# Preparing the first row tiles of a layer's attention within the last expert tiles of the layer before

## The chip, the cores and the metric

The kernel runs on one core of one Trainium2 chip, in one launch. The metric is the device time in microseconds of that core, the median of the timed runs. A profile of one execution by the hardware profiler stands beside it; its engines are TensorE (PE, with its weight loads as PEld), VectorE (DVE), ScalarE (ACT), GpSimd (POOL) and the DMA queues of SyncE (SP) and GpSimd. "Granted clock" is the share of TensorE's full clock that the chip grants: in this profile 1.00 (2.4 GHz) or 0.50 (1.2 GHz).

## What is computed

Two decoder-like layers on x of 4 x 1024 x 256 with a context of 4 x 77 x 256, in float32. Layer 0 is a cross attention and a mixture of experts; layer 1 a cross attention and a low-rank feed forward.

```python
def reference(x, ctx_1024, ...):
    x = x + _L0_xattn_ref(_layernorm(x), ctx_1024, ctx_1024, ...)
    x = x + _L0_ffn_ref(_layernorm(x), router_w, w1, w2)     # 8 experts, 2 chosen for a row, hidden 1024, gelu
    x = x + _L1_xattn_ref(ctx_1024, ctx_1024, _layernorm(x), ...)
    x = x + _L1_ffn_ref(_layernorm(x), U1, V1, b1, U2, V2, b2)
    return x

def _L1_xattn_ref(values, keys, query, Wv, Wk, Wq, Wo, bo):   # 16 heads of 16
    ...
    energy = jnp.einsum('nqhd,nkhd->nhqk', q, k)
    attention = jax.nn.softmax(energy / jnp.sqrt(jnp.float32(EMBED)), axis=-1)
    out = jnp.einsum('nhql,nlhd->nqhd', attention, v).reshape(N, Lq, EMBED)
    return out @ Wo.T + bo
```

## The kernel before

The 4096 rows of x are 32 row tiles of 128 (`NT`), eight for each of the four batches (`TB`). The function `experts_and_attend` holds layer 0's experts and layer 1's attention as one block: each engine runs its own written order of work, and semaphores join them. There is no planner; the order is that of the loops.

**Expert tiles.** Rows are gathered by expert. After seven short tiles come 32 full tiles (`FULL`) of 256 rows, `step(t)` on each engine. On TensorE one is four groups `up(0..3)` of twelve matmuls of 256 columns, two groups `down`, the transposes of the next tile's rows (`rows_turned`), and two more groups `down`. ScalarE applies the gelu to each up group (L1787) and copies the result y out (L1802); VectorE splits each activation into a high and a low half (L1908, L1910) and the turned rows too (L1897). GpSimd gathers the rows of a tile two tiles ahead (L1381), SP stores y (L1460).

**Row tiles of the attention.** The result of the experts for row tile f is two gathers from the stored y by GpSimd (`gather(f)`, L1406), a load of x by SP (L1465), and VectorE's `rows_in_full(f)`: two weighted additions, then mean and variance (L1969 to L1979). The gathers of rows 0 to 7 need only what the first tiles stored; `gather(TB)`, row 8, waits for the store of the last expert tile. GpSimd computes the deviation (`deviation(f)`, L1413, L1416), ScalarE normalizes (`normed_rows`, L1831), TensorE transposes (`rows_transposed`, L1692), ScalarE and VectorE keep the high and low halves (`high` L1825, `low` L1984). Then come four score matmuls of 308 columns (`scores(f, i)`, L1622), 16 heads in all, of which VectorE takes the maxima over the keys. The maxima of four row tiles make a group; they are scaled (L2002), transposed (`maxima_transposed`, L1631) and copied (L1858).

`SOON_ROWS` = 6 row tiles (`AHEAD`) are prepared up to `low` within expert tiles 25 to 31: `LED` is 25, `rows_in_full` of row t - 25 and the transposes of row t - 26 stand in tile t. X of these six has its own place; X of the others lies in the area of the experts' weights.

**The steps.** `STEPS` runs k from -5 to 32. Step k in 0 to 31 takes one quarter of a group g = k // 4: `scores_by_key(k)` (L1653, three terms, then the maxima as a fourth), the exponentials `exps(k, 0)` and `exps(k, 1)` by ScalarE (L1837), and in the next step `values` (L1665) and their copy (L1843). Beside this run the scores of row k + 5 (from row 5 on), `rows_in_full(k + 7)`, the normalization and transposes of row k + 6, and, from step 5 on, the heads and the projection of row k - 5. Steps -5 to -1 hold only the scores of rows 0 to 4 (`EARLY`), all four into the four banks of `sT_ps`, one reduction over all four by VectorE (`early_maxima`, L1994), and ten matmuls of `awake` (L1698), which compute nothing and keep TensorE occupied. Steps 0 to 4 have twelve `awake` matmuls each. On ScalarE, `normed_rows(k + 6)` stands in front of `exps(k, 0)`; on VectorE `rows_in_full(k + 7)` stands between reductions 1 and 2 of row k + 5.

The tail of GpSimd's order is:

```python
for t in range(LED, FULL):
    f = t - LED
    if f >= 3:
        deviation(f - 3)
    step(t)
    gather(f)
gather(SOON_ROWS + 1)
for f in range(FULL - LED - 3, SOON_ROWS):
    deviation(f)
```

and after it, for each row f from 6 on: `gather(f + 2)`, `deviation(f)`, and from f = 8 on the bias of row f - 8. So the gathers of row 8 stand ahead of the deviation of row 6.

## Time and profile before

| | us |
|---|---|
| median of three timed runs | 1009.81 |
| lowest and highest | 1009.03, 1011.61 |
| the profiled execution | 1009.16 |
| its span | 1007.2 |
| TensorE busy (share) | 918.5 (91%) |
| VectorE busy | 616.9 (61%) |
| ScalarE busy | 513.6 (51%) |
| GpSimd busy | 423.6 (42%) |

How to read it: the span is what the profiler saw from the first to the last instruction, and the execution's own time lies 2 us above it. Busy times overlap, and they are averages over stages with different limits; TensorE's matmuls are pipelined and their ends modelled, so the distance from one start to the next tells the cost of one in a row of them, and the duration (longer) doesn't. In a timeline the columns are start, duration, engine, line and operation, output and inputs with their shapes, the count of instructions merged into the row, and in brackets the idle time of the engine just before it and what ended that.

### The profile page before, as it was taken

Reading aid. Unit: us, or ns where it says so; the run is one execution under the profiler, and the core shown is the slowest. Engines: PE = TensorE matmul, PEld = TensorE weight load, DVE = VectorE, ACT = ScalarE, POOL = GpSimd, SP = SyncE. Lnnn points to the kernel's source line nnn. Section 1 sums busy time; section 2 is a strip of 40 time slices with the busy share of each in tenths; the row PEclk is TensorE's granted clock in tenths of the full one; section 3 lists DMA queues with packets and bytes.
Section 4 is the critical chain, followed back from the end, with each engine's and each line's share of the span. In section 5 each row is a group of like instructions: output and inputs, shape, how many; then the busy total and the mean of one; then the engine's idle time right before and its main releaser. Section 6 shows DMA issues by size and latency. Waiting matters only on the chain. (4 is left out here: it accounts for less than half of the span.)

```text
span 1007.2 us, 24069 instructions
## 1 busy us (share of the span) xinstructions
PE 918.5 (91%) x8072; PEld 641.0 (64%) x8072; DVE 616.9 (61%) x1502; ACT 513.6 (51%) x872; POOL 423.6 (42%) x575
## 2 busy tenths in 40 slices
PE   5799999998269999999999999999799999989995
PEld 3555656554136799889899889999544444444552
DVE  4477888875896344445455444565668888545661
ACT  1478888886352433333333333344257667645663
POOL 2487777771201113333433322453256665204550
PEclk9999999999778999999999999999979999999998
DMA  6323444425521111211111111232124221000112
GB/s 190 76 84 93 127 130 130 135 85 168 186 98 53 48 43 43 64 44 43 52 55 43 49 59 54 74 95 75 42 80 108 74 75 48 2 1 17 49 47 59
DMA packets 73729, 75.45 MB, mean 75 GB/s; under 512 B 22730, under 2 KB 66874, under 8 KB 73626
## 3 DMA queue, kind: packets, MB, share of 16 engines
q1 hardware_dynamic: 67146, 56.31, 18.7%
q0 software_dynamic: 6480, 17.70, 6.5%
q8 instruction: 73, 1.20, 0.5%
q14 instruction: 30, 0.25, 0.1%
HBM read 51.64 MB, written 22.34 MB: 73 GB/s over the span
## 5 line engine op out<-in xcount | busy, mean ns | idle before, releaser
L1908 DVE CAST hh_e<-h_e 128x512 f16<-128x512 f32 x128 | 57.9, 452 | 166.4 <-ACT h_e L1787 92.7
L1575 PE MATMUL banks_ea<-experts,hh_e 128*128 x512 | 139.6, 273 | 0.0
L1574 PE MATMUL banks_ea<-experts,hh_e 128*128 x512 | 139.6, 273 | 0.0
L1561 PE MATMUL banks_ea<-xT_e,experts 128*128 128x256 f16 x512 | 139.6, 273 | 0.0
L1576 PE MATMUL banks_ea<-experts,hh_e 128*128 x512 | 139.6, 273 | 0.0
L1562 PE MATMUL banks_ea<-xT_e,experts 128*128 128x256 f16 x512 | 139.6, 273 | 0.0
L1560 PE MATMUL banks_ea<-xT_e,experts 128*128 128x256 f16 x512 | 139.6, 273 | 0.0
L1787 ACT ACTIVATE h_e<-banks_ea 128x512 f32<-128x512 f32 x128 | 76.5, 597 | 85.0 <-PE banks_ea L1562 85.0
L1910 DVE TENSOR_TENSOR hh_e<-h_e,hh_e 128x512 f16<-128x512 f32 x128 | 88.6, 692 | 4.4
L1381 POOL DMA_INDIRECT x_e<-xh_scratch,token x29 | 32.3, 1113 | 135.1 <-PE banks_ea L1501 90.8
L1837 ACT ACTIVATE experts<-banks_ea 77x1024 f32<-77x1024 f32 x64 | 64.9, 1016 | 44.5 <-PE banks_ea L1653 44.5
L625 POOL TENSOR_TENSOR experts<-keys,blocks 128x616 f16<-128x616 f16 x64 | 76.6, 1218 | 0.0
L1406 POOL DMA_INDIRECT w_late<-y_scratch,slots_t x64 | 63.1, 987 | 29.0 <-issue 16.3
L1378 POOL COPY idx_e<-token 128x2 int32 x21 | 12.9, 612 | 133.5 <-PE banks_ea L1501 133.5
L835 ACT ACTIVATE experts<-sT_ps 77x1024 f32<-77x1024 f32 x64 | 65.1, 1017 | 7.3 <-PE sT_ps L694 4.2
L1777 ACT ACTIVATE xT_e<-banks_ea 128x512 f16<-128x512 f32 (+1 forms) x39 | 21.7, 558 | 89.8 <-PE banks_ea L1501 89.8
L1988 DVE TENSOR_REDUCE experts<-banks_ea 128x4 f32<-128x308 f32 x108 | 50.9, 471 | 17.2 <-PE banks_ea L1622 16.3
L2311 ACT ACTIVATE experts<-h_ps_f,experts 128x512 f32<-128x512 f32 x64 | 43.3, 689 | 30.1 <-PE h_ps_f L2253 30.1
L928 DVE TENSOR_REDUCE qcat<-s_ps 128x8 f16<-128x616 f32 x64 | 51.1, 798 | 8.5 <-PE s_ps L720 4.3
L1802 ACT ACTIVATE y_e<-banks_ea 128x256 f32<-128x256 f32 x64 | 21.1, 381 | 67.0 <-PE banks_ea L1576 67.0
L1562 PEld LDWEIGHTS banks_ea<-xT_e,experts 128*128 x512 | 50.1, 98 | 5.8
L1575 PEld LDWEIGHTS banks_ea<-experts,hh_e 128*128 128x128 f16 x512 | 50.1, 98 | 5.8
(367 smaller groups left out, 2202.7 us busy)
## 6 DMA issues: line engine op xcount, KB each, us to landing
experts<-in_L_ffn_w SPq DMA_DIRECT2D x22, 512.0 KB, 4.3
y_scratch<-y_e SPq DMA_DIRECT2D x32, 256.0 KB, 3.3
x<-in_x SPq DMA_DIRECT2D x32, 128.0 KB, 3.2
experts<-in_x SPq DMA_DIRECT2D x64, 64.0 KB, 2.5
x_scratch<-x SPq DMA_DIRECT2D x16, 256.0 KB, 2.5
xh_scratch<-xn SPq DMA_DIRECT2D x16, 256.0 KB, 2.8
w_late<-in_L_ffn_w SPq DMA_DIRECT2D x8, 512.0 KB, 4.4
w_late<-x_scratch SPq DMA_DIRECT2D x32, 128.0 KB, 2.5
```

The source lines that it names most:

```text
L625: nc.gpsimd.tensor_tensor(bd[:, f % 2, flat(i, 2), :, :], G["khi"][0][:, b, heads].rearrange("p (q k) -> p q k", q=2)[:, :, None, :] .broa ...
L835: nc.scalar.activation(prob[:, k % 2, qh, :, :], sT_ps[0:KEYS, :, :], ACT.Exp).then_inc(exp_ok, 1)
L1406: pool.indirect_dma_start(out=rows[:, f % 4, :], out_offset=None, in_=A["y"][0:EARLY_ROWS, :] if f < TB else A["y"], in_offset=bass.Indire ...
L1560: mm(out, w[0], xT[0][:, c, :], start=c == 0, stop=False)
L1561: mm(out, w[0], xT[1][:, c, :], start=False, stop=False)
L1562: last = mm(out, w[1], xT[0][:, c, :], start=False, stop=c == DC - 1)
L1574: mm(out, a[0], w[0], start=m == 0, stop=False)
L1575: mm(out, a[0], w[1], start=False, stop=False)
L1576: last = mm(out, a[1], w[0], start=False, stop=m == 7)
L1787: nc.scalar.activation(h[:, q % 2, :], up_ps[q], ACT.Gelu, scale=1 / WSCALE).then_inc(gelu_ok, 1)
L1837: nc.scalar.activation(prob[:, k % 2, 2 * half:2 * half + 2, :], sT_ps[0:KEYS, 2 * half:2 * half + 2, :], ACT.Exp, scale=1.0 / 16).then_in ...
L1910: nc.vector.tensor_tensor(hh[1][own], h[own], hh[0][own], ALU.subtract).then_inc(hlo_ok, 1)
```

## The change

`SOON_ROWS` becomes 8. `LED` is then 23: rows 0 to 7 are put together in expert tiles 23 to 30 and transposed in 24 to 31 (`TURNED`). Rows 0 to 6 (`EARLY`) have their scores and maxima in expert tiles 25 to 31 (`SCORED`): the four matmuls stand between the up and down groups, all into the one bank that holds the transposed rows too, and each waits until VectorE has reduced the one before it. The maxima of group 0 are scaled in tile 28 and transposed in tile 31, and the steps begin at k = 0. GpSimd computes the deviations of rows 6 and 7 ahead of the gathers of rows 8 and 9. X of rows 6 and 7 takes the place of three tables of constants that only the router reads; the maxima take that of router logits and of the experts' gathered rows. ScalarE computes one exponential of a single column behind the last copy of y. TensorE waits for the last copies of y only at the scores of row 7.

```diff
-        STEPS = range(-5, QUARTERS + 1)
+        STEPS = range(QUARTERS + 1)
-        EARLY = range(5)
+        EARLY = range(7)
+        TURNED, SCORED = LED + 1, LED + 2
...
                     step(t)
-                    gather(f)
-                gather(SOON_ROWS + 1)
+                    if f < SOON_ROWS:
+                        gather(f)
                 for f in range(FULL - LED - 3, SOON_ROWS):
                     deviation(f)
+                for f in range(SOON_ROWS, SOON_ROWS + 2):
+                    gather(f)
...
+                    scored = t - SCORED
                     pe.wait_ge(xlo_ok, SH + t + 1)
+                    if scored == 0:
+                        pe.wait_ge(k1_ok, 2 * B * DC)
                     up(0)
+                    if scored in EARLY:
+                        scores(scored, 0)
                     up(1)
...
                     up(2)
+                    if scored in EARLY:
+                        scores(scored, 1)
                     up(3)
+                    if scored in EARLY:
+                        scores(scored, 2)
                     down(0)
+                    if scored in EARLY:
+                        scores(scored, 3)
                     down(1)
                     if t + 1 < FULL:
                         rows_turned(SH + t + 1)
-                    if t - LED - 1 in AHEAD:
-                        rows_transposed(t - LED - 1)
+                    if t - TURNED in AHEAD:
+                        rows_transposed(t - TURNED)
+                    if t + 1 == FULL:
+                        pe.wait_ge(xlo_ok, SH + FULL)
+                        maxima_transposed(0)
                     down(2)
                     down(3)
...
-                    after(pe, max_ok, 4 * f if f in EARLY else 4 * f + i)
-                    mm(sT_ps[:, i, 0:CH] if f in EARLY else s_ps[:, 0:CH], xhi[f // 4 % 3][:, i // 2, flat(f % 4, P)],
+                    if f in EARLY and i == 0:
+                        pe.wait_ge(lo_ok, f + 1)
+                    if f == len(EARLY) and i == 0:
+                        pe.wait_ge(y_ok, SH + 2 * FULL)
+                    after(pe, max_ok, 4 * f + i)
+                    mm(t_bank[:, 0:CH] if f in EARLY else s_ps[:, 0:CH], xhi[f // 4 % 3][:, i // 2, flat(f % 4, P)],
                        G["khi"][1][:, b, ds(4 * i * KEYS, CH)], start=True, stop=True).then_inc(s_done, 1)
...
                 def rows_transposed(f):
                     pe.wait_ge(xh_ok, f + 1)
                     after(pe, lo_ok, f)
+                    after(pe, max_ok, 4 * min(f, len(EARLY)))
...
-                pe.wait_ge(k1_ok, 2 * B * DC)
                 pe.wait_ge(gelu_ok, FIRST_Q + QS * FULL)
-                pe.wait_ge(xlo_ok, SH + FULL)
-                pe.wait_ge(y_ok, SH + 2 * FULL)
                 for k in STEPS:
                     f, n = k + 5, k - 5
                     filled = 0 <= k < 5
                     if tile(n):
                         heads_out(n, k)
-                    if f in EARLY:
-                        awake(2)
-                        for i in range(4):
-                            scores(f, i)
-                        awake(8)
...
+                if isinstance(t, int) and t + 1 == FULL:
+                    nc.scalar.activation(early[:, :], G["neghalf"][:, :], ACT.Exp)
...
                         nc.vector.tensor_tensor(hh[1][own], h[own], hh[0][own], ALU.subtract).then_inc(hlo_ok, 1)
+                        if isinstance(t, int) and t - SCORED in EARLY:
+                            for i in ((0,), (1, 2), (3,), ())[q]:
+                                maximum(t - SCORED, i)
...
+                    if isinstance(t, int) and t - SCORED == 3:
+                        maxima(0)
...
-SOON_ROWS = 6
+SOON_ROWS = 8
```

## Rows read from the trace of the kernel before

**Rows 1.** The head of the page.
```profile
span 1007.2 us, 24069 instructions
```
**Rows 2.** Windows, around the end of the experts: stretch, length, busy us (instructions) by engine, clock, DMA.
```profile
core 0: us, PE busy (x) PEld busy (x) DVE busy (x) ACT busy (x) POOL busy (x), PEclk, DMA share, GB/s
700.00:709.50 9.50, 9.43 (x86) 8.04 (x84) 4.81 (x9) 3.29 (x7) 0.27 (x1) 1.00 0.13 41
709.50:722.40 12.90, 9.12 (x74) 6.81 (x75) 8.34 (x9) 1.18 (x3) 1.98 (x2) 1.00 0.14 42
...
727.00:731.00 4.00, 2.05 (x20) 0.81 (x21) 2.25 (x6) 2.73 (x5) 3.34 (x5) 0.98 0.38 119
731.00:734.00 3.00, 3.00 (x14) 0.70 (x13) 1.73 (x6) 1.18 (x2) 0.94 (x3) 0.50 0.31 87
...
742.00:746.00 4.00, 3.34 (x33) 1.90 (x34) 2.42 (x7) 2.47 (x5) 3.25 (x5) 1.00 0.12 35
```
**Rows 3.** Timeline of TensorE, steps -5 to 3.
```profile
710.49 0.69 PE L1622 MATMUL banks_ea<-keys,w_late 128*128 128x308 f16 x4
711.01 1.25 PE L1698 MATMUL banks_ea<-keys,ident 128*128 128x256 f16 x10
712.87 0.69 PE L1622 MATMUL banks_ea<-keys,w_late 128*128 128x308 f16 x4 [0.61 <-DVE experts L1994]
...
721.42 0.39 PE L1631 MATMUL banks_ea<-ident,experts 128*128 128x128 f16 x4
...
726.15 0.38 PE L1692 MATMUL banks_ea<-const,kc 128*128 128x128 f32 x2
726.37 0.60 PE L1698 MATMUL banks_ea<-keys,ident 128*128 128x256 f16 x4
...
746.23 1.05 PE L1665 MATMUL banks_ea<-experts,v_sb 77*17 77x512 f32 x8
```
**Rows 4.** Timeline of ScalarE, from the last copy of y to step 5.
```profile
709.47 0.66 ACT L1802 ACTIVATE y_e<-banks_ea 128x256 f32<-128x256 f32 x2 [2.30 <-PE banks_ea L1576]
...
725.09 0.60 ACT L1831 ACTIVATE kc<-experts,shift_a,rstd_a 128x256 f32<-128x256 f32 x1 [2.65 <-POOL shift_a L1416]
725.71 1.28 ACT L1837 ACT_TABLE_LOAD   x1
727.00 1.93 ACT L1837 ACTIVATE experts<-banks_ea 77x1024 f32<-77x1024 f32 x2
...
739.98 1.02 ACT L1837 ACTIVATE experts<-banks_ea 77x1024 f32<-77x1024 f32 x1 [3.70 <-PE banks_ea L1653]
...
745.79 1.02 ACT L1837 ACTIVATE experts<-banks_ea 77x1024 f32<-77x1024 f32 x1 [1.47 <-PE banks_ea L1653]
...
756.39 1.02 ACT L1837 ACTIVATE experts<-banks_ea 77x1024 f32<-77x1024 f32 x1 [1.48 <-PE banks_ea L1653]
```
**Rows 5.** Timeline of VectorE: one expert tile's casts, then step 0.
```profile
656.11 0.43 DVE L1908 CAST hh_e<-h_e 128x512 f16<-128x512 f32 x1 [1.28 <-ACT h_e L1787]
...
657.41 0.43 DVE L1908 CAST hh_e<-h_e 128x512 f16<-128x512 f32 x1 [0.16 <-ACT h_e L1787]
...
660.78 0.43 DVE L1908 CAST hh_e<-h_e 128x512 f16<-128x512 f32 x1 [2.21 <-PE banks_ea L1576]
...
662.09 0.43 DVE L1908 CAST hh_e<-h_e 128x512 f16<-128x512 f32 x1 [0.16 <-PE banks_ea L1576]
...
722.18 0.47 DVE L1969 SCALAR_TENSOR_TENSOR wp<-w_late,cw_t 128x256 f32<-128x256 f32 x1
...
723.95 0.47 DVE L1988 TENSOR_REDUCE experts<-banks_ea 128x4 f32<-128x308 f32 x1
```
**Rows 6.** Timeline of GpSimd behind the experts; last, the gathers' landing over the kernel.
```profile
713.08 1.04 POOL L1406 DMA_INDIRECT w_late<-y_scratch,slots_t  x1 [12.72 <-DMA y_scratch<-y_e]
714.43 0.94 POOL L1406 DMA_INDIRECT w_late<-y_scratch,slots_t  x1 [0.31 <-issue]
724.12 0.56 POOL L1413 TENSOR_TENSOR rstd_a<-ve_a,neghalf 128x1 f32<-128x1 f32 x1 [8.75 <-DVE ve_a L1979]
...
DMA to landing us min/median/max: 2.7/3.0/4.8
```

More of the change, by code:

```diff
@@ L59 @@
 _at = 0
[L60 removed]
+for _n, _w in (("ident", P), ("tri", P), ("rowid", P), ("restart", E * NT), ("halfid", HALFT), ("blocks", P // HD),
                ("rows", 3),
[L62 removed]
+               ("share", P // HR * 2), ("mrows", 4), ("tokenid", 2 * NT), ("rank8", E), ("unit1", ET),
                ("early", P), ("latekeys", HEADS * KEYS), ("latekey", KEYS), ("queryid", 2 * 2 * 8 * 5)):
@@ L1789, in step @@
                             short_result(SH - 1)
-                    f = t - LED - 1 if isinstance(t, int) else -1
+                    f = t - TURNED if isinstance(t, int) else -1
                     if f in AHEAD:
@@ L1910, in step @@
                         nc.vector.tensor_tensor(hh[1][own], h[own], hh[0][own], ALU.subtract).then_inc(hlo_ok, 1)
+                        if isinstance(t, int) and t - SCORED in EARLY:
+                            for i in ((0,), (1, 2), (3,), ())[q]:
+                                maximum(t - SCORED, i)
                     if not isinstance(t, int) or t + 1 < FULL:
                         rows(SH + t + 1)
-                    if isinstance(t, int) and t - LED - 1 in AHEAD:
-                        low(t - LED - 1)
+                    if isinstance(t, int) and t - TURNED in AHEAD:
+                        low(t - TURNED)
                     if isinstance(t, int) and t - LED in AHEAD:
                         rows_in_full(t - LED)
+                    if isinstance(t, int) and t - SCORED == 3:
+                        maxima(0)
                 def link(ins):
@@ L2043, in _ @@
                     step(t)
+                nc.vector.memset(mcat[:, :, :], 0.0)
                 for t in range(LED, FULL):
@@ L2048, in _ @@
                 dve.wait_ge(down_done, FIRST_DOWN + QS * FULL)
-                nc.vector.memset(mcat[:, :, :], 0.0)
                 nc.vector.memset(v_ps, 0.0).then_inc(v_ok, 1)
@@ L2152, in allocate_last @@
     G["nc"], G["lent"] = nc, Q
-    soon, rest = L.sb("X_soon", [P, SOON_ROWS, D]), Q.sb("X", [P, NT - SOON_ROWS, D])
+    own, rest = SOON_ROWS - 2, Q.sb("X", [P, NT - SOON_ROWS, D])
+    soon = L.sb("X_soon", [P, own, D])
+    used = G["const"][:, CC["tri"][0]:CC["restart"][1]].rearrange("p (n d) -> p n d", d=D)
     def rows(n, count=1):
-        part, at = (soon, n) if n < SOON_ROWS else (rest, n - SOON_ROWS)
+        part, at = (soon, n) if n < own else (used, n - own) if n < SOON_ROWS else (rest, n - SOON_ROWS)
         return part[:, at, :] if count == 1 else part[:, at:at + count, :]
```

21 lines of the change are left out of this document (6 added, 15 removed).

## The prediction

> **What bounds the kernel now.** I read the page first, then the windows around the place that the change touches, then each engine's timeline there. The profiled execution took 1009.16 us, of which 1007.2 are its span [rows 1]; the median of the three timed runs is 1009.81, so 0.65 is added to a sum made against the profile. In the last expert tiles TensorE has no gap: in 700.0 to 709.5 it is busy 9.43 of 9.50 us at the full granted clock [rows 2], so whatever is added to its queue there lengthens the span by its own time. The last expert tile ends where ScalarE may copy its result, at 709.47 [rows 4]; I call this moment E. From there to the first steady step stands a stretch that no engine fills. TensorE is busy 9.12 of 12.90 us [rows 2], and much of that is matmuls of `awake`, which compute nothing. The five preparation steps k = -5 to -1 are a strict exchange: four score matmuls (0.52 us from the first start to the next group), ten awake matmuls, then idle 0.61 us until VectorE's reduction has freed the banks, and this again every 2.38 us (710.49 to 712.87) [rows 3]. They end with the transposes of the maxima at 721.42 [rows 3], E+11.95.
>
> Step k=0 then isn't free either. VectorE prepares row tile 6 from 722.18 and reaches the first reduction of row 5 at 723.95 [rows 5]; GpSimd computes the deviation of row 6 at 724.12, behind the gathers of row 8, which began at 713.08 after the last store of the experts [rows 6]; ScalarE normalizes row 6 at 725.09, having waited 2.65 us for it, loads the exponential's table (1.28 us) and starts the exponentials of k=0 only at 727.00, E+17.53 [rows 4]. In 727 to 731 TensorE is busy 2.05 of 4.00 us, after which its granted clock is 0.50 [rows 2], the lower of the two levels; it is 1.00 again in 742 to 746 [rows 2]. So the exponentials of k=2 start at 739.98, those of k=3 at 745.79, those of k=5 at 756.39 [rows 4]. From here the steps come 5.2 to 5.3 us apart; I take k=5, at E+46.92, as the marker: behind it both kernels do the same work.
>
> **The change, part by part.** *1. The preparation leaves the path.* Steps -5 to -1 are gone with their 50 awake matmuls. The scores of rows 0 to 6, the transposes of rows 6 and 7, and the maxima of group 0 are done inside expert tiles 24 to 31. What remains of it for TensorE lies on the path, since it is full there. Scores: 7 tiles x 4 matmuls, 0.52 us for four [rows 3], is 3.64. Two more pairs of row transposes: 0.22 each (726.15 to 726.37) [rows 3], 0.44. The four transposes of maxima: 0.39 at most [rows 3], 0.25 taken since ends are modelled longer than spacing. Together 4.3 us.
>
> *2. New waits in the tiles.* Scores now share one bank, so each of the four waits for VectorE's reduction of the one before (about 0.47 us, a row of 128x308). I laid a tile out from its rows. VectorE's cast of quarter 1 has waited 0.16 us for ScalarE, so the first reduction pushes it by 0.3 us, and the reduction's release is still there well before the next score, which stands two quarters later on TensorE. Before quarter 2 VectorE waits 2.21 us for TensorE [rows 5]; reductions 1 and 2 (0.95 us) fit in it. The fourth delays quarter 3's cast, which has only 0.16 us [rows 5], by 0.15 to 0.3 us; the last down group needs that quarter about 0.6 us later than it is there. `rows_transposed` waits for this fourth reduction too: I get a tenth of slack where x is turned between, and 0.35 us of stall in the last tile, where nothing is. I take 0.7 for the seven tiles; the bounds are 0 and 0.5 per tile, 3.5. Parts 1 and 2 add 5.0 us before E, with ends 4.3 and 7.8. On ScalarE the two further normalizations and on VectorE the two further row preparations go into idle time that the seven or so tiles have on both (VectorE waits 1.28 and 2.21 us in one [rows 5]).
>
> *3. k=0 and k=1.* All their inputs are there. TensorE no longer waits for the copies of y but begins the scores by key at once, behind the table load. ScalarE: two copies 0.66, table load 1.28 [rows 4], a one-element exponential, estimated 0.2, between nothing and the 0.56 of GpSimd's one-column power [rows 6]: exponentials of k=0 at E+2.2, done E+4.1 (1.93 for the pair) [rows 4]. Step 1's scores follow them in 1.2 us (ScalarE waits 1.47 for such scores with one reduction between them [rows 4]); exponentials at E+5.4; the values, 1.05 us at the full clock [rows 3], put their copy at E+7.0; the second exponential ends at E+8.4. The table load is still exposed here, since y's copy precedes it and nothing else does: what was saved is that it no longer follows row 6. On this load the Trainium skill says more ("ScalarE: Activation LUTs", "What ACT_TABLE_LOAD costs"): that every switch costs a drain of some 1.4 us on top. The row disagrees: the load of 1.28 us at 725.71 is followed by the exponential at 727.00 [rows 4]. By the page k=0 would be later by that drain, but k=2 below would not.
>
> *4. k=2 has a new last wait: row 8.* Its gathers need the last store of the experts and can't move ahead. They begin, as before, at E+3.61 and E+4.96 (713.08, 714.43), and the second lands 3.0 us after its issue [rows 6]: E+7.96. VectorE's five operations on the row take 1.77 us (722.18 to 723.95) [rows 5]: E+9.8. Queued behind this wait on VectorE is the first reduction of row 7, without which TensorE can't go on in k=2. GpSimd goes through the gathers of rows 9 and 10 first, four at about 1.3 us, until E+11.2; then the deviation of row 8 (0.56 for the power [rows 6], half that for the shift), E+12.0; ScalarE's normalization, 0.6 us, stands in front of the exponentials of k=2: E+12.6. Before, that was 739.98, E+30.51. The deviations of rows 6 and 7 now precede the gathers and run behind expert tiles.
>
> *5. From k=2 to k=5.* Before: 16.41 us (739.98 to 756.39), its start still at the low clock. After, at the full clock: 4.5 us to k=3 and twice 5.3 (half of 745.79 to 756.39 [rows 4]), 15.1; GpSimd's two gathers for a row, its deviation and its bias fit in that. The clock, though: TensorE in the new stretch idles about 1.8 us in E+2.4 to E+4.2 (awake matmuls of k=0 done, exponentials not), 0.7 before k=2 and 1.3 in it. That is as thin as the stretch before 731, after which the clock fell [rows 2]. I expect it to fall once for about the same 10 us. Costs by walking through with TensorE's work doubled: about 1.8 us if it falls at k=1, where row 8 is waited for anyway, 3.5 if at k=2. I take 2.8.
>
> *Sum.* Marker k=5: before E+46.92. After 12.6 + 15.1 + 2.8 = 30.5, so 16.4 less; E itself 5.0 later; net 11.4. 1009.16 - 11.4 = 997.8; with 0.65, 998.4. New SBUF places (maxima and X of rows 6 and 7 in tables that the router has done with) cost nothing that a row shows: the widths are unchanged. The later loads of x on the SP queue keep their distance to the rows. The zeroing of `mcat` moves into a tile's idle time.
>
> **Rivals.** *A. The clock doesn't fall.* For: 24 awake matmuls remain in k=0 and 1 alone. Against: the idle times above. Gives 2.8 more: 995.6. *B. The second batch's row chain holds k=2 to k=4.* Row 8 to 10 come one behind another through GpSimd with no reserve, where they had been prepared behind the old five steps. A gather's landing took up to 4.8 us where the median is 3.0 [rows 6]; 1 to 1.8 us more for each of three rows gives 3 to 5: 1001.5 to 1003.5. Against: VectorE and GpSimd are nearly idle then. *C. Handshakes partly exposed,* 1 us in each of seven tiles: 1005.4. Against: the slack of part 2. *D, slower:* the exchange of scores and reductions comes into the open in the full tiles. A reduction of 0.47 and the 0.61 us that TensorE waited after one [rows 3] make 1.1 per score, 4.3 a tile, 30 in seven: about 1028. It decides from a stall of 2.1 us a tile (11.4 net gain and 3, over seven). It needs reductions that regularly stand behind a VectorE operation which itself waits for TensorE; only the fourth does, and its wait ends just then. *E. GpSimd late beside VectorE.* It issues the gathers of x and y and the deviations in the same tiles while VectorE gets 1.9 us more work in each; a late deviation stalls the transposes in TensorE's full queue, about 0.5 a tile, 1002. The Trainium skill names such a mechanism ("SBUF — State Buffer", "Who interferes with whom"): the two engines lock a port pair against each other. But the reductions read the accumulation banks, one input.
>
> **How the numbers follow.** Chances: forecast (996.5 to 1000.5) 0.52, A 0.15, B 0.14, C 0.07, E 0.05, D 0.04, no effect from another cause 0.03. The range takes in A, B and E and the bound of the stalls: 994.5 to 1004. A measurement of this kernel tells 0.3% (3 us) from no change. Faster by more than that (below 1006.8) 0.91, within it 0.04, slower 0.05.
>
> **What would show it.** The end of the experts 4 to 6 us later with TensorE still unbroken, 0.52 us per tile, and no idle before scores; exponentials of k=0 two us behind the y copies; those of k=2 about 12.6 us behind, ScalarE waiting for GpSimd's shift; one fall of the clock; k=5 30.5 us after the experts. Wrong it would be if TensorE waits for reductions within tiles, if gathers of row 8 land later than 8 us, or if rows 9 to 11 are waited for too.

## The result, and the profile after

The changed kernel took 1000.79 us, the median of four runs (995.99 to 1003.9), against 1010.11 (1009.03 to 1011.61) for the kernel before: a ratio of 0.9906, with a 95% interval of 0.9886 to 0.9926, or 7.5 to 11.5 us less. The forecast was 998.4 with a range of 994.5 to 1004. In the same measurement as three other experiments (`rows8_only`, `dev_first`, `awake_fill`, below) the unchanged text of the changed kernel, `again`, took 996.27 (995.08 to 1001.67, six runs), ratio 0.9882 (0.9859 to 0.9905). Its ten runs scatter over 8.8 us (995.08 to 1003.9), where seventeen of the kernel before in one measurement scatter over 4.3 (1007.87 to 1012.13), and this has to be taken apart before single microseconds of it mean anything.

So I read every trace by the same marks. **First** is the start of ScalarE's first copy of y in the first full expert tile, **E** that of the last, **k0 to k5** the starts of the first exponentials of steps 0 to 5 counted from E, and **rest** what the span has behind k5. My table of these, from ScalarE's timelines:

| kernel | first | tiles (E - first) | k0 | k1 | k2 | k3 | k4 | k5 | rest | span |
|---|---|---|---|---|---|---|---|---|---|---|
| before | 370.11 | 339.36 | 17.53 | 21.48 | 30.51 | 36.32 | 41.62 | 46.92 | 250.81 | 1007.2 |
| after | 375.05 | 344.80 | 2.08 | 5.23 | 12.64 | 17.06 | 25.15 | 30.44 | 251.61 | 1001.9 |
| again | 370.68 | 344.81 | 2.07 | 5.22 | 12.69 | 17.10 | 22.40 | 27.70 | 250.41 | 993.6 |
| after - before | +4.94 | +5.44 | -15.45 | -16.25 | -17.87 | -19.26 | -16.47 | -16.48 | +0.80 | -5.3 |
| again - before | +0.57 | +5.45 | -15.46 | -16.26 | -17.82 | -19.22 | -19.22 | -19.22 | -0.40 | -13.6 |

The two heads, after first; the rows that answer to these are [rows 1] and the page's table of busy times. The numbers behind the engines are busy time, share of the span and instructions; PEclk is the granted clock of TensorE in 40 slices of the span, in tenths.

```profile
span 1001.9 us, 23945 instructions
PE 918.6 (92%) x8022; PEld 640.7 (64%) x8022; DVE 616.3 (62%) x1517; ACT 513.4 (51%) x873; POOL 422.1 (42%) x573
PEclk9999999999876999999999999999989999999998
```

```profile
span 993.6 us, 23945 instructions
PE 909.3 (92%) x8022; PEld 636.1 (64%) x8022; DVE 615.9 (62%) x1517; ACT 512.9 (52%) x873; POOL 422.3 (43%) x573
PEclk9999999999877999999999999999999999999998
```

Both ran the same instructions. What differs is how long TensorE took for its own: 918.6 against 909.3 us. Three places make up the 8.3 us of span between them: 4.4 ahead of the first full tile, 2.7 between k3 and k4, 1.2 behind k5.

Windows of after around E, to be held against [rows 2] (columns: stretch, its length, busy time and instructions by engine, clock, DMA share, GB/s):

```profile
core 0: us, PE busy (x) PEld busy (x) DVE busy (x) ACT busy (x) POOL busy (x), PEclk, DMA share, GB/s
690.00:719.70 29.70, 29.35 (x267) 25.68 (x264) 20.36 (x45) 10.59 (x22) 4.03 (x6) 1.00 0.13 37
719.70:722.20 2.50, 2.50 (x30) 1.49 (x28) 0.48 (x1) 2.32 (x5) 0.00 (x0) 1.00 0.29 102
722.20:724.00 1.80, 0.04 (x5) 0.04 (x5) 0.00 (x0) 1.64 (x2) 0.55 (x1) 1.00 0.02 5
724.00:727.40 3.40, 3.40 (x37) 1.68 (x37) 0.00 (x0) 1.78 (x3) 2.49 (x4) 1.00 0.26 77
727.40:731.00 3.60, 2.18 (x24) 0.86 (x21) 2.83 (x8) 0.74 (x1) 2.98 (x4) 1.00 0.51 146
737.00:740.00 3.00, 3.00 (x15) 0.68 (x14) 1.69 (x7) 1.28 (x2) 2.58 (x4) 0.50 0.34 102
```

The last two and a half tiles keep TensorE busy 29.35 of 29.70 us. Behind E there is no exchange of 12.9 us any more but 2.5 us of work (scores by key, awake), a gap of 1.8 until the exponentials of k=0 free their input, step 1, and a thin 3.6 us while row 8 is waited for. In 737 to 740 the clock is 0.50.

ScalarE, after, from a tile to step 5 (start, duration, engine, line and operation, tiles, count, and in brackets the idle time before and what ended it); it answers to [rows 4]:

```profile
660.80 0.66 ACT L1817 ACTIVATE y_e<-banks_ea 128x256 f32<-128x256 f32 x2 [2.08 <-PE banks_ea L1580]
672.56 0.66 ACT L1817 ACTIVATE y_e<-banks_ea 128x256 f32<-128x256 f32 x2 [2.08 <-PE banks_ea L1580]
...
719.85 0.66 ACT L1817 ACTIVATE y_e<-banks_ea 128x256 f32<-128x256 f32 x2 [1.97 <-PE banks_ea L1580]
720.53 1.28 ACT L1819 ACT_TABLE_LOAD   x1
721.82 0.20 ACT L1819 ACTIVATE experts<-neghalf 128x1 f32<-128x1 f32 x1
721.93 1.91 ACT L1854 ACTIVATE experts<-banks_ea 77x1024 f32<-77x1024 f32 x2
...
731.99 0.60 ACT L1848 ACTIVATE kc<-experts,shift_a,rstd_a 128x256 f32<-128x256 f32 x1 [3.84 <-POOL shift_a L1418]
732.49 1.00 ACT L1854 ACTIVATE experts<-banks_ea 77x1024 f32<-77x1024 f32 x1
...
736.91 1.02 ACT L1854 ACTIVATE experts<-banks_ea 77x1024 f32<-77x1024 f32 x1 [0.22 <-PE banks_ea L1673]
...
745.00 1.02 ACT L1854 ACTIVATE experts<-banks_ea 77x1024 f32<-77x1024 f32 x1 [1.11 <-PE banks_ea L1673]
...
750.29 1.02 ACT L1854 ACTIVATE experts<-banks_ea 77x1024 f32<-77x1024 f32 x1 [1.48 <-PE banks_ea L1673]
```

A tile with scores takes 672.56 - 660.80 = 11.76 us. Exponentials of k=0 stand 2.08 us behind the copies of y; those of k=2 start half a microsecond behind a normalization that waited 3.84 us for GpSimd's shift. From k=3 (736.91) to k=4 (745.00) it is 8.09 us instead of 5.3: the stretch with the low clock.

What comes ahead of that shift, on VectorE and on GpSimd, after; the first rows of VectorE are in the last tile, the others answer to [rows 5, 6]:

```profile
714.88 0.43 DVE L1925 CAST hh_e<-h_e 128x512 f16<-128x512 f32 x1 [0.90 <-PE banks_ea L1580]
...
715.95 0.47 DVE L2010 TENSOR_REDUCE lx<-banks_ea 128x4 f32<-128x308 f32 x1
...
727.55 0.48 DVE L1991 SCALAR_TENSOR_TENSOR wp<-w_late,cw_t 128x256 f32<-128x256 f32 x1 [6.38 <-DMA w_late<-y_scratch,slots_t]
...
729.34 0.47 DVE L2010 TENSOR_REDUCE lx<-banks_ea 128x4 f32<-128x308 f32 x1
```

```profile
723.45 1.04 POOL L1408 DMA_INDIRECT w_late<-y_scratch,slots_t  x1 [14.04 <-DMA y_scratch<-y_e]
724.80 0.95 POOL L1408 DMA_INDIRECT w_late<-y_scratch,slots_t  x1 [0.30 <-issue]
...
729.80 0.95 POOL L1408 DMA_INDIRECT w_late<-y_scratch,slots_t  x1 [0.30 <-issue]
730.76 0.83 POOL L1415 TENSOR_TENSOR rstd_a<-ve_a,neghalf 128x1 f32<-128x1 f32 x1
731.69 0.27 POOL L1418 TENSOR_SCALAR shift_a<-mv_a,rstd_a 128x1 f32<-128x1 f32 x1
```

The first gather of row 8 is issued at 723.45, E+3.60; VectorE has its rows at 727.55, E+7.70; GpSimd gets to the deviation at 730.76, once the gathers of rows 9 and 10 are issued, and the shift begins at E+11.84.

### The profile page after: what moved, and what is told of

Its sections match the earlier page's. It is cut to its first block and busy times, and to the rows that moved or that the text cites. A ratio compares the mean times of both kernels' runs of the same rounds, so it can differ in the third digit from the quotient of the medians.

```text
span 1001.9 us, 23945 instructions
## 1 busy us (share of the span) xinstructions
PE 918.6 (92%) x8022; PEld 640.7 (64%) x8022; DVE 616.3 (62%) x1517; ACT 513.4 (51%) x873; POOL 422.1 (42%) x573
## 5 line engine op out<-in xcount | busy, mean ns | idle before, releaser
L1383 POOL DMA_INDIRECT x_e<-xh_scratch,token x33 | 36.8, 1114 | 151.5 <-PE banks_ea L1505 105.5
L2010 DVE TENSOR_REDUCE lx<-banks_ea 128x4 f32<-128x308 f32 x128 | 60.3, 471 | 18.5 <-PE banks_ea L1644 18.0
```

## The experiments

**Theory.** Both halves are as the forecast had them: the tiles are 5 us longer by TensorE's own work, and behind E the wait for row 8 stands last in k=2, through GpSimd's queue. **Rivals:** the clock is what moves the time, not the steps; or the tiles are longer by handshakes; or the gain comes from preparing rows 6 and 7 and not from the removal of the five steps. For a fall of the clock there was the additional question whether the changed kernel has it always.

### The same kernels again, and the scatter

`again` and `before_again` have no edit.

> The changed kernel once more, nothing edited, for its spread and for a second profile. Two theories of its first profile, in which the first full expert tile already ended 4.94 us later than before (375.05 against 370.11) in code that the change doesn't touch but for the order of the table of constants. Theory 1, chance: the part ahead of the experts varies from execution to execution; the second profile's first copy of y may lie anywhere between 369 and 376, and the marker (exponentials of step 5 behind the last copies of y) is 30.4 again, 28 to 31 by where the clock falls. Theory 2, the new order of constants or the longer written-out part costs it: the first copy of y is near 375 again and the median near 1001 to 1003. By theory 1 the median is 997 to 1001.

> The kernel before once more, nothing edited, for a second profile. Theory: its fall of the clock 21 us behind the last copies of y belongs to its pattern, two steps with TensorE half idle behind steps with awake matmuls; it is there again for about 10 us, and step 5 lies 46.9 behind the copies. Rival, chance as in the changed kernel: no fall, step 5 at about 43.5; then 3.4 us of the first comparison are chance.

Measured: `again` 996.27 us, just below the expected 997 to 1001, with the profile shown above; its low clock behind E is absent, and k5 stands at 27.70 rather than 30.44, just below the expected 28 to 31. ScalarE of `again` at steps 2 to 5:

```profile
728.18 1.00 ACT L1854 ACTIVATE experts<-banks_ea 77x1024 f32<-77x1024 f32 x1
...
732.59 1.02 ACT L1854 ACTIVATE experts<-banks_ea 77x1024 f32<-77x1024 f32 x1 [0.21 <-PE banks_ea L1673]
...
737.89 1.02 ACT L1854 ACTIVATE experts<-banks_ea 77x1024 f32<-77x1024 f32 x1 [1.00 <-PE banks_ea L1673]
...
743.19 1.02 ACT L1854 ACTIVATE experts<-banks_ea 77x1024 f32<-77x1024 f32 x1 [1.48 <-PE banks_ea L1673]
```

The second profile of the kernel before (1008.95 us) repeats the first at every mark within 0.2 us, the 10.24 us of low clock from E+21 included (k5 at 46.89, tiles 339.35). So in the kernel before the fall behind E came in both profiles; in the changed one it came in one of two.

The early part explains most of the rest of the scatter. The first exponentials of the first layer begin at 58.0 (before), 60.8 (after) and 58.3 (again); and around the router the clock is low in two stretches of 17.1 or 20.5 us each: 17.1 and 20.5 in before, 20.5 and 20.5 in after, 17.1 and 17.1 in again.

Over the traces of the changed kernel and its variants **first** lies between 370.68 and 375.05, in no order that follows an edit, but it does follow the clock: where the low stretches ahead of it sum to 37.6 us it is 370.68 to 370.97 (`again`, `turn_late`, `no_awake`), where they sum to 41.0 or 44.4 it is 372.3 to 373.0 (`dev_first`, `dev8_first`, `no_store_wait`), and at 47.8 it is 373.8 to 373.9 (`scores_twice`, `no_early_exp`, `best3`). After and `awake_fill` (44.4 us; 375.05 and 374.86) began the first layer's exponentials some 2.4 us later besides (60.8 and 60.4, the others at 57.8 to 58.7). Behind **first** the tiles of all unedited ones agree within 0.01 us. Of the 1.2 us behind k5, after shows one more short low stretch, 3.4 us from k5+126.6, that `again` lacks (`scores_twice` and `no_awake` have one too, and a rest of 251.8 and 251.6).

The ten executions of the changed kernel go the same way as their mean granted clock: the six of 995.08 to 997.56 us had 0.977 or 0.978, the four of 998.8 to 1003.9 had 0.968 to 0.973. So medians of few runs tell less than the marks, and I judge single microseconds by marks.

### Rows 6 and 7 alone

The kernel before, with eight rows prepared in the tiles but the five steps kept:

```diff
-SOON_ROWS = 6
+SOON_ROWS = 8
...
-                    gather(f)
-                gather(SOON_ROWS + 1)
+                    if f < SOON_ROWS:
+                        gather(f)
                 for f in range(FULL - LED - 3, SOON_ROWS):
                     deviation(f)
+                for f in range(SOON_ROWS, SOON_ROWS + 2):
+                    gather(f)
```

and X of rows 6 and 7 in the used constants, as in the change.

> One part of the change alone: rows 6 and 7 too are put together and transposed within the expert tiles, and the deviations of rows 6 and 7 stand ahead of the gathers of rows 8 and 9, but the steps -5 to -1 with their scores and awake matmuls stay as before. Theory: the last copies of y come 0.4 to 0.5 us later than before; the maxima's transposes still 12 us behind them; the exponentials of step 0 no longer wait for row 6, 15.3 instead of 17.5; row 8 is ready by then, so step 2 waits for nothing; marker step 5 at 40.5 without a fall of the clock and 43 with one, 46.9 before. Time 3.5 to 6 below before. Rival: the preparation of rows 6 and 7 was most of what the change brings, then the marker is under 36 and the time 9 below before.

Measured: 1004.39 us (1001.92 to 1007.19, ten runs), ratio 0.9946 (0.993 to 0.9962). Tiles 339.80, 0.44 more: exactly the two pairs of transposes. k0 at 14.62 (15.3 expected), k5 at 39.58 (40.5), no low clock up to k5. So of the 19.2 us that `again` has at k5, rows 6 and 7 give 7.3 (46.92 to 39.58): 2.9 ahead of k0 and 4.4 between k0 and k5, where the fall is missing. How much of the 4.4 comes from rows 6 and 7 and how much from the missing fall isn't separated. The removal of the five steps gives 11.9 (39.58 to 27.70), and its price in the tiles is 344.81 - 339.80 = 5.0. Both parts are gains; the rival that only rows 6 and 7 matter is out.

### What the scores in the tiles cost

Each early score's matmul is issued twice:

```diff
-                    mm(t_bank[:, 0:CH] if f in EARLY else s_ps[:, 0:CH], ...,
-                       ...).then_inc(s_done, 1)
+                    for again in range(2 if f in EARLY else 1):
+                        last = mm(t_bank[:, 0:CH] if f in EARLY else s_ps[:, 0:CH], ...,
+                                  ...)
+                    last.then_inc(s_done, 1)
```

> The changed kernel with each of the 28 score matmuls in the expert tiles issued twice, the same result twice. Theory: TensorE is full there, so a score matmul costs its distance from start to start, 0.13 us: from the first copy of y to the last 344.80 + 3.6 = 348.4 us. Rival, that the distance is ruled by the exchange with VectorE, whose slack takes up the second matmul: under 346. Above 349.5 if the fourth reduction, a tenth late in every tile already, stalls TensorE further.

Measured: 1001.78 us, tiles 347.72, 2.91 more for 28 matmuls, 0.104 each. The full price of 0.13 would be 3.6. So some 0.7 went into waits that were there anyhow. The steps from one copy of y to the next show it: without scores in the tile 11.13 us (`rows8_only`), with eight score matmuls 12.18, which is 11.13 and eight times 0.13 with nothing left over; with four 11.77 (after), which is 0.11 more than four times 0.13. Where the waits are the groups of TensorE's instructions in 640 to 720 of after tell in part (count, busy us, mean ns, idle before and what ended it), and its timeline, the transposes of a row in a middle tile and in the last one:

```profile
L1644 PE MATMUL banks_ea<-keys,w_late 128*128 128x308 f16 x27 | 7.9, 294 | 0.0
...
L1713 PE MATMUL banks_ea<-const,kc 128*128 128x128 f32 x14 | 2.9, 286 | 0.4 <-DVE lx L2010 0.4
```

```profile
704.28 0.60 PE L1505 MATMUL banks_ea<-const,x_e 128*128 128x128 f32 x4
704.80 0.41 PE L1713 MATMUL banks_ea<-const,kc 128*128 128x128 f32 x2
...
716.56 0.41 PE L1713 MATMUL banks_ea<-const,kc 128*128 128x128 f32 x2 [0.35 <-DVE lx L2010]
```

None of the scores waits. In the last tile nothing stands between the down groups and the transposes, and these wait 0.35 us for the fourth reduction (715.95 to 716.4 on VectorE above), since they go into the same bank. In the others x of the next tile is turned in between, and no idle time shows. The next kernel moves the transposes behind one more down group:

```diff
-                    if t - TURNED in AHEAD:
-                        rows_transposed(t - TURNED)
                     if t + 1 == FULL:
...
                     down(2)
+                    if t - TURNED in AHEAD:
+                        rows_transposed(t - TURNED)
                     down(3)
```

> The changed kernel with the transposes of a row tile one down group later in the expert tile (between the last two groups). Theory: what the tiles cost above the pure time of the added matmuls (5.44 against 4.3 us) is the wait of these transposes for the fourth reduction, about 0.1 in each tile and 0.35 in the last; placed 1.3 us later they don't wait, and from the first copy of y to the last it is 343.9 instead of 344.80. Rival: VectorE's low half and the row preparation move back by up to 1.3 us and push the first cast of the next tile; then 344.8 or more.

Measured: tiles 343.62, 1.19 less than `again`, and k5 unchanged (27.63); 998.16 us (994.25 to 1000.17, four runs). So the tiles' 5.45 are: 28 scores at 0.13, 3.64; two pairs of transposes, 0.44; the maxima, some 0.2; and 1.2 of stall. From one copy of y to the next the six tiles 25 to 30 take 11.66 us in `turn_late` and 11.77 in after, the last tile 11.45 and 11.99: 0.11 in each of six, too short for a row of its own, and 0.54 in the last, of which the row above shows 0.35.

### What k=2 waits for

Two causes are in series there: the store of the last y must land before row 8 can be gathered, and GpSimd issues the gathers of rows 9 and 10 ahead of row 8's deviation. The first is taken away by letting rows 8 to 11 gather early rows' slots:

```diff
-                    if f == TB:
+                    if f == TB + 4:
                         pool.wait_ge(y_out, stored(FULL))
-                    b, s = f // TB, f % TB
+                    b, s = f // TB if f >= TB + 4 else 0, f % TB
```

(and the same bound, TB + 4, for the table that is gathered from). The outputs of these rows are then other rows' sums.

> The changed kernel in which the gathers of rows 8 to 11 take the slots of rows 0 to 3, so that they need nothing of the last expert tiles and don't wait for the last store (the outputs of these rows are then other rows' sums). It prices the wait that took the place of those removed. Theory: rows 8 and 9 lie ready before the last copies of y; the exponentials of step 2 come 9.8 behind these copies instead of 12.6, those of step 5 25.4 instead of 27.7 (unbroken clock). Rival: GpSimd's and VectorE's work on row 8 is the bound, not its data; then step 2 stays above 11.5.

Measured: k2 at 9.90 instead of 12.69, k5 at 25.80 instead of 27.70; 995.77 us, ratio 0.9854 (0.9835 to 0.9874). The last wait of k=2 is then the scores of TensorE. So row 8 costs 2.8 us at k=2, of which 1.9 are left at k=5, and from k2 on the steps come 5.3 apart.

The second cause is taken away by putting the deviation ahead, for every row or for row 8 alone:

```diff
                 for f in range(SOON_ROWS, NT):
+                    deviation(f)
                     if f + 2 < NT:
                         gather(f + 2)
-                    deviation(f)
```

```diff
                 for f in range(SOON_ROWS, NT):
+                    if f == SOON_ROWS:
+                        deviation(f)
                     if f + 2 < NT:
                         gather(f + 2)
-                    deviation(f)
+                    if f > SOON_ROWS:
+                        deviation(f)
```

> The changed kernel with GpSimd computing the deviation of row f ahead of the gathers of row f + 2 (from row 8 on), nothing else. Theory: in step 2 the last wait is the four gather issues in front of row 8's deviation, so its shift comes at 10.7 behind the last copies of y instead of 12.1, the exponentials of step 2 at 11.2 instead of 12.64, and of step 3 about 1 earlier; marker 29.4 instead of 30.4 if the clock falls once as before. In the steady steps nothing changes, since GpSimd idles 1.2 us a step there. Rival: the data of row 8 (landing, VectorE) is the last wait, then step 2 stays at 12.6; or the later gathers of rows 10 and up are now late and steps 4 and 5 lose 1 us each.

> The changed kernel with the deviation of row 8 alone ahead of the gathers of row 10; from row 9 on the order is as in the change. When every deviation stood ahead, the exponentials of step 2 came 11.3 behind the last copies of y instead of 12.7, but the steps behind took 5.6 instead of 5.3, with GpSimd's addition of the bias beside VectorE's two additions (0.73 and 0.83 us instead of 0.48 each). Theory, that this meeting is the cause: step 2 at 11.3, step 5 at 26.7 with an unbroken clock (29.5 with one fall), and from step 5 to the end 250.4 again; 1 us faster than the change. Rival: later gathers are the cause; then row 10's gathers, which are still later here, cost 1 us or more before step 5.

Measured: `dev_first` 1002.3 us (1001.42 to 1003.73), k2 at 11.27 and k5 at 26.80, but rest 256.76: 0.9 us won up to k5, 6.3 lost behind it, 6.0 of them between the exponentials of k=5 and k=31. The expectation had no such loss. `dev8_first` 997.22 (996.96 to 997.74), k2 at 11.22, rest 250.38, but k3 at 17.93 and k5 at 27.65. So the queue cost 1.4 us at k=2. Where the order is changed for row 8 only, the same wait appears a step later, in the row of ScalarE's second normalization here:

```profile
728.48 0.60 ACT L1851 ACTIVATE kc<-experts,shift_a,rstd_a 128x256 f32<-128x256 f32 x1 [2.41 <-POOL shift_a L1418]
...
735.19 0.60 ACT L1851 ACTIVATE kc<-experts,shift_a,rstd_a 128x256 f32<-128x256 f32 x1 [3.32 <-POOL shift_a L1418]
```

Row 9's deviation stands behind the gathers of rows 10 and 11; nothing was left at k5. And the loss of `dev_first` behind k5 is a meeting of two engines. Groups of instructions in 745 to 840 (name, count, then busy us, mean ns of one, idle before), `dev_first` first, `again` second:

```profile
L1994 DVE SCALAR_TENSOR_TENSOR experts<-w_late,cw_t,wp 128x256 f32<-128x256 f32 x18 | 14.7, 816 | 0.6
L1424 POOL TENSOR_TENSOR experts<-experts,bo_a 128x256 f32<-128x256 f32 x13 | 12.5, 964 | 0.3
L1991 DVE SCALAR_TENSOR_TENSOR wp<-w_late,cw_t 128x256 f32<-128x256 f32 x17 | 11.4, 669 | 0.0
```

```profile
L1424 POOL TENSOR_TENSOR experts<-experts,bo_a 128x256 f32<-128x256 f32 x14 | 10.2, 726 | 0.0
L1994 DVE SCALAR_TENSOR_TENSOR experts<-w_late,cw_t,wp 128x256 f32<-128x256 f32 x18 | 8.7, 485 | 0.6
L1991 DVE SCALAR_TENSOR_TENSOR wp<-w_late,cw_t 128x256 f32<-128x256 f32 x18 | 8.5, 475 | 0.0
```

With the deviation ahead, GpSimd's addition of the bias falls beside VectorE's two operations that combine a row, and all three are longer: 816 for 485 ns, 669 for 475, 964 for 726. Some 0.5 us a step on VectorE, and most steps come 5.5 to 5.7 apart instead of 5.2 to 5.4. VectorE is busy 84.0 of these 95 us in `again` already (TensorE 90.4), and TensorE's scores wait for its reductions 5.9 us in `dev_first`, 3.2 in `again`. The Trainium skill has a rule that fits ("SBUF — State Buffer", "Who interferes with whom"): a VectorE instruction with two inputs in SBUF contends with a GpSimd instruction that reads SBUF. The trace agrees in kind, with 0.19 and 0.33 us per instruction of VectorE and 0.24 of GpSimd. `dev8_first`, which keeps the later steps' order and has its rest back, shows that this order is the cause, but not by which of its effects. That it is the meeting, `dev_first` itself shows: once in this window the addition comes later and meets neither operation, and all three have their old length:

```profile
788.87 0.48 DVE L1991 SCALAR_TENSOR_TENSOR wp<-w_late,cw_t 128x256 f32<-128x256 f32 x1
789.38 0.48 DVE L1994 SCALAR_TENSOR_TENSOR experts<-w_late,cw_t,wp 128x256 f32<-128x256 f32 x1
...
790.25 0.74 POOL L1424 TENSOR_TENSOR experts<-experts,bo_a 128x256 f32<-128x256 f32 x1
```

The step around it takes 5.18 us (exponentials at 788.81 and 793.99), as in `again`. The sixteen other pairs of the window all overlap an addition and are all longer. The expectation's rival, gathers that come too late, doesn't show: VectorE waits 0.0 us ahead of the first of the two operations there.

### The clock

The unedited kernel showed the fall once in two profiles. Two kernels change how much TensorE is kept occupied. `awake_fill` adds such matmuls where it waits; `no_awake` takes those of steps 0 to 2 away:

```diff
                         if term == 3:
+                            if k in (2, 3):
+                                awake(8)
...
+                    if k == 3:
+                        awake(10)
...
-                        awake(4)
+                        awake(16 if k == 0 else 4)
```

```diff
+                    filled = 3 <= k < 5
                     if filled:
```

> The changed kernel with more awake matmuls where TensorE was idle: 12 more in step 0, 8 ahead of the last term in steps 2 and 3, 10 at the start of step 3. Theory: the fall of the clock at 736.9, three steps in, costs 2.8 us (8.09 instead of 5.3 from step 3 to step 4); with the idle time filled it doesn't fall: clock 1.00 throughout, step 3 to 4 takes 5.3, marker 27.7 to 28.5. Rival: the added matmuls delay the scores that are waited for by 0.9 us each and the clock falls all the same: marker 31 to 32.

> The changed kernel without the awake matmuls of steps 0 to 2 (36 of them; those of steps 3 and 4 stay). It makes TensorE thin behind the experts on purpose, to see the fall of the clock that my prediction counted on and that one of six profiles of such kernels showed. Theory: the clock falls within steps 1 to 3 in every execution, low for 7 to 10 us, and step 5 comes at 29.5 to 31 instead of 27.7. Rival: the thin stretch is too short for it; without a fall the missing matmuls save nothing, 27.3 to 27.7.

Measured: `awake_fill` 1000.01 us (998.46 to 1001.62), no fall, k5 at 28.47, but k3 at 17.88 instead of 17.10: the added matmuls cost 0.8, and since `again` had no fall either, they bought nothing in this profile. `no_awake` 999.33 us, k5 at 29.22 (29.5 to 31 expected), and its windows from E on:

```profile
715.78:720.78 5.00, 1.82 (x32) 0.77 (x30) 0.48 (x1) 3.96 (x6) 1.10 (x2) 1.00 0.15 52
720.78:725.78 5.00, 3.68 (x25) 0.70 (x21) 2.12 (x6) 2.52 (x3) 3.78 (x5) 0.53 0.42 117
725.78:734.78 9.00, 7.80 (x43) 2.14 (x39) 5.68 (x14) 4.53 (x7) 7.82 (x11) 0.50 0.30 87
734.78:739.78 5.00, 4.56 (x45) 2.32 (x45) 3.00 (x10) 3.08 (x7) 3.78 (x6) 1.00 0.30 93
```

TensorE busy 1.82 us in the first 5 behind E, then clock 0.50 for 13.7 us in all (E+5 to E+19). No profile with these empty matmuls shows a fall so early, so they seem to keep the clock there; one profile without them is all there is for it. A fall that early, with the time that the missing matmuls give back, costs only 1.5 us at k5, because its first 7.3 us lie ahead of k2, which comes at 12.66 as in `again`: there row 8 is waited for anyway. A fall at k=3, as in after, costs 2.7.

### The table load

The single-column exponential is dropped:

```diff
-                    if isinstance(t, int) and t + 1 == FULL:
-                        nc.scalar.activation(early[:, :], G["neghalf"][:, :], ACT.Exp)
```

> The changed kernel without the one-column exponential behind the last copies of y. Theory: ScalarE has nothing else to do there and the first scores by key are ready 1.0 behind the start of the copies, so the table is loaded 0.3 us later, the exponentials of step 0 start at 2.3 to 2.4 instead of 2.08, and as row 8 is waited for in step 2 anyway nothing is left of it: step 2 at 12.6, step 5 at 27.7 (unbroken clock). Rival: the early load hides the whole 1.28 us; then step 0 starts at 3.2 or later.

```profile
718.64 0.66 ACT L1817 ACTIVATE y_e<-banks_ea 128x256 f32<-128x256 f32 x2 [1.97 <-PE banks_ea L1580]
719.32 1.28 ACT L1852 ACT_TABLE_LOAD   x1
720.61 1.93 ACT L1852 ACTIVATE experts<-banks_ea 77x1024 f32<-77x1024 f32 x2
```

Measured: k0 at 1.97, 0.1 earlier than with it (2.08); the expectation, 2.3 to 2.4, missed. The load starts right behind the copies either way, 0.68 us behind the start of the first; it doesn't wait for what the exponential waits for: the last score matmuls ahead of the exponential start at 719.21 and end, by their modelled ends, at 719.6, the load has started at 719.32. The extra instruction costs 0.1 us and brings nothing. (998.59 us, one run; its k5 is 27.63.)

### A version from these findings

Deviations ahead for rows 8 and 9 only, the bias two rows later (`LAG`), so that it doesn't fall beside VectorE's row, and the transposes as in `turn_late`:

```diff
-                KN, LAG = 2 * B * DC, 8
+                KN, LAG = 2 * B * DC, 10
...
+                    soon = f < SOON_ROWS + 2
+                    if soon:
+                        deviation(f)
                     if f + 2 < NT:
                         gather(f + 2)
-                    deviation(f)
+                    if not soon:
+                        deviation(f)
```

> The changed kernel with three edits: the transposes of a row tile stand between the last two down groups; the deviations of rows 8 and 9 stand ahead of the gathers of rows 10 and 11, and from row 10 on the order is the change's; the bias is added ten rows behind instead of eight, so that GpSimd doesn't add one in the first steps. With the deviation of row 8 alone moved, step 2 came at 11.22 but step 3 at 17.93, as GpSimd was in debt by one row when it reached row 9's deviation. Theory: GpSimd's queue is what holds steps 2 and 3; step 2 at 11.2, step 3 at 16.1, step 5 at 26.7 with an unbroken clock, 250.4 from there to the end, tiles 343.6: 2.2 us less than the change where both have no fall of the clock, median 994.5 to 995.5. Rival: the debt falls on row 10 (its deviation behind the gathers of row 12), then step 4 comes at 22.2 or more and only the tiles' 1.2 us are left.

Measured: tiles 343.61, k2 11.21, k5 26.66, rest 250.42, all three effects together, and the three groups of the meeting are at 485, 475 and 724 ns (485, 475 and 726 in `again`): 2.24 us less than `again` from the first full tile on. Its time was 996.5 us (996.44 to 996.8, four runs; 994.5 to 995.5 expected), ratio 0.9864 (0.9848 to 0.9881), where `again` had 0.9882 (0.9859 to 0.9905): lower, with intervals that overlap. The profiled execution had **first** at 373.81, 3.13 later than that of `again`. So the gain of 2.2 us is shown by the marks; by the times alone it isn't told from nothing.

## Why the prediction was right, step by step

*Parts 1 and 2, the tiles.* Forecast 5.0 (4.3 and 0.7), measured 5.44 and 5.45. The scores are what they should be: a tile with eight is 8 times 0.13 us longer than one with none (`scores_twice`, `rows8_only`), so that 28 of them cost 3.64 as forecast; `rows8_only` gives 0.44 for the two pairs, as forecast. The stalls were mis-sized: 1.2 instead of 0.7 (`turn_late`). The forecast's 0.35 in the last tile is the idle time before its transposes to the digit, but `turn_late` takes away 0.54 there; what was sized as "a tenth of slack" in the six others is a tenth of stall (0.11). Rivals C (1 us a tile) and D (4.3 a tile) didn't come: the reductions 1 to 3 fit in where they were laid out, since none of the 27 scores in the groups' row waits. (The forecast's 1005.4 for C and 1028 for D are added to a sum that holds the 0.7 of stalls already; they should be 0.7 less.)

*Part 3, k=0 and k=1.* Forecast E+2.2 and E+5.4, measured 2.08 and 5.23. The single-column exponential took 0.20, of which 0.1 is in sequence. On the table load the forecast set the row (1.28 us) against the Trainium skill's drain of some 1.4 us ("ScalarE: Activation LUTs", "What ACT_TABLE_LOAD costs"): again the next activation starts 1.29 us behind the load's start, in after and in `no_early_exp`. The trace shows no drain behind it.

*Part 4, k=2.* Forecast E+12.6, measured 12.64 and 12.69, and by the forecast's way: gathers of row 8 at E+3.60 (3.61), landed at E+7.70 (7.96), GpSimd's queue free at E+10.9 (11.2), ScalarE idle 3.84 us for the shift. That the sizes inside were off by 0.3 in both directions (the deviation took 0.83 us instead of 0.56) evened out. `no_store_wait` and `dev8_first` separate the causes: 1.4 us are the queue, 1.3 more the store and the gather. Rival B, that rows 9 and 10 would be late too, didn't come in the unedited kernel (k2 to k3 4.4 us), but `dev8_first` shows it sat right behind: moving one deviation brought k2 1.5 us forward and put k3, which waits for row 9, 0.8 later than in `again`.

*Part 5, k=2 to k=5.* Without a fall, forecast 15.1, measured 15.01 (`again`). With one, forecast 2.8 more, measured 2.79 more (17.80, after). The size of the term is right, in part by luck: the forecast took the middle between the costs of a 10 us fall at k=1 (1.8) and at k=2 (3.5), and what came was one of 6.8 us at k=3. And that the clock falls, the forecast's likeliest case, came in one of the nine profiles of the changed kernel and of those variants that leave the awake matmuls alone. Of these, seven have an edit elsewhere, so the one in two of the unedited kernel is the direct evidence, and one in nine the wider one. Rival A, given 0.15, seems to be what most executions do: 995.6 by the forecast, 996.27 measured, and six of the ten executions have the mean clock of `again`'s profile within 0.001. The forecast took the thin stretch before 731 [rows 2] as a model for the new one; that stretch repeats its fall in both profiles of the kernel before, the new one doesn't.

*The sum.* Against k5 the forecast had -16.4 and -11.4 net. After shows -16.48 at k5 and -11.04 net of the tiles, `again` -19.22 and -13.77. The one thing that isn't in the sum is the early part: **first** at +4.94 in after and +0.57 in `again`. It lies ahead of everything but the order of the constants' table, and since `again` has the same order, that order isn't the cause of the 4.4 between them. The forecast had no term for such scatter, and its lower end, 994.5, took in times like `again`'s only because rival A was in the range. So the marks of after agree with the forecast to 0.5 us, with a fall of the clock that came by chance, and its profiled execution lies 5.5 above the forecast, of which 4.94 lie ahead of the first full tile. That the median of 1000.79 is 2.4 above the forecast for the same reason isn't shown, since the other three executions have no profile. Open remains what sets the length of the clock's low stretches ahead of **first**, and why two executions began 2.4 us later; no experiment here addressed it.

*The other costs at nothing.* The later loads of x on the SP queue and the new places in SBUF cost nothing that a mark shows (rest 250.41 against 250.81). Rival E, GpSimd late beside VectorE in the tiles, didn't come there, but `dev_first` showed the same mechanism behind k5, at 6.3 us. That the deviations of rows 6 and 7 must go ahead of the gathers of rows 8 and 9 was not tried the other way round: these gathers wait for the last store, which comes behind tiles that need those rows transposed, and by the code that would never end.

## What to carry over

Work that is moved into a full engine's queue costs its issue distance, and here that was right to 10%; what remains to be found is each place where it shares a bank, since the stall is removed by moving the consumer one group of matmuls later. When a prologue is taken away, look for the first row that could not be moved, follow it through every queue that it passes (a store, two gathers, another row's gathers, a deviation), and expect that a cure for one row hands the wait to the next. And when two profiles of one kernel differ, compare them from mark to mark before comparing medians: 8.3 us between two traces of the same code came from three places, none of them in what the change had moved into the tiles.

## What the chip showed that was not expected

- The clock's fall behind E is nearly reproducible in one kernel (at E+21, for 10.24 us, twice of two) and comes by chance in another: 6.8 us in after, none in `again`. It cost 2.7 us at k=3, but a fall of 13.7 us from E+5 on cost 1.5 (`no_awake`, net of the matmuls left out), since its first half lay in a wait.
- VectorE's operations with two inputs and GpSimd's addition slow each other when they meet (means 485 to 816, 475 to 669 and 726 to 964 ns), enough to lengthen a step by 0.3 us, though TensorE is the busiest engine of the stage (90.4 of 95 us, VectorE 84.0). In the one row of the window that doesn't meet, the lengths are 0.48, 0.48 and 0.74 us.
- The table load is not held by the operands of the activation behind it: it started 0.68 us after the copies began, with or without an early exponential.
- A GpSimd power of one column, 0.56 us elsewhere [rows 6], took 0.83 in after at 730.76, while VectorE ran the two operations with two inputs of row 9. These weren't longer for it (0.48 each), so it isn't plain that it is the same meeting; nothing was done to find out.
